# Router logits with the weights stationary, and the last batch of cross-attention interleaved with its output projections, in a Flamingo block kernel on Trainium2

## The chip, the cores and the metric

The kernel runs on one core of a Trainium2 chip. TensorE (PE) multiplies matrices, VectorE (DVE) and ScalarE (ACT) do elementwise work, GpSimd (POOL) does a little of it and issues the DMAs with computed addresses, SyncE (SP) issues the other DMAs. Each engine works off its own queue in order and meets the others only through semaphores. The metric is the time of one execution on the device in microseconds (us); lower is better. The kernel before takes 1012.65 us, the median of three runs (1010.91 to 1013.94).

## What is computed

Eight sequences of 112 tokens (896 tokens, 512 features) pass through four stages, each on a layernorm of x and added to x with a tanh gate:

```
x += tanh(g_xattn[0]) * softmax cross-attention over a context of 8 x 375 rows,
                        output projected with Wo, scaled, layernormed again (gamma, beta)
x += tanh(g_ffn[0])   * (silu(h @ gate.T * gate_s) * (h @ up.T * up_s)) @ down.T * down_s      # inner size 1408
x += tanh(g_xattn[1]) * linear attention: (q kv_summary) / (q k_sum) * sigmoid gate, @ Wo.T
# mixture of experts; t is the layernorm of x
scores = softmax(t @ gate_w.T)            # 16 experts
weights, indices = top_k(scores, 2)
y = sum over experts of swiglu(t; w1[e], w3[e], w2[e]) * weight       # inner size 352
z = swiglu(t; sw1, sw3, sw2)                                          # shared, inner size 704
x += tanh(g_ffn[1]) * (y + z)
```

## The kernel before

**Products.** Operands are split into a high and a low part in a rounded float32 type, and `product` (lines 536 to 543) issues three matmuls for each of the four chunks of 128 features: high by high (L540), high by low (L541), low by high (L542). So one projection of 128 tokens on 512 features is 12 matmuls with 512 moving columns, and one `gate_up` of half the tokens is 12 matmuls with 448. The high part of an operand is a copy by ACT, the low part a subtraction by DVE. The few plain float32 products (L620, L801, L900, L908, L932) each appear in the trace as two matmul instructions.

**First attention, batch by batch.** For each batch b of the loop, PE computes scores for four groups of heads (L603), values (`values_0`), the keys and values of the second attention (`keys_1`, `values_1`), the mix of probabilities and values (L620) and `kv_summary` (L589). DVE clips the scores (`clip`, L1382), ACT exponentiates them (`exps`), DVE normalises the mix (`normalise`, L1389 to L1395) and splits the result into hT (`heads_low`, L1399). The next score product on PE waits for the clip before it, since both use the same PSUM banks. For batches 0 to 6 the tile `k1` lies over the tiles 4 to 6 of x; so after the last `kv_summary`, SP loads these three tiles of x again (`x_again`), and POOL then adds the beta row to them (L1744).

**The last batch** (line 740 on) is written out by hand, with the output projections of the seven token tiles put between its pieces: `to_tokens(t, output_of_0)`, called y0 to y6 here. y0 to y5 need batches 0 to 6 only, y6 needs batch 7 (`ct_sv`). In order PE runs: scores 0, three values_0, scores 1, keys_1 0, y0, mix 0, values_1 0, scores 2, keys_1 1, y1, mix 1, values_1 1, y2, scores 3, keys_1 2, mix 2, values_1 2, y3, mix 3, kv_summary, y4, y5, y6, transposes of tiles 0 to 3 for the first feed-forward, and the first gate_ups with the transposes of tiles 4 to 6 between them. For each projected tile DVE runs `delta` (L1442 to L1446: scale, bias, statistics), ACT a square root (`delta_std`), DVE `residual` (L1452 to L1455 and the statistics L1282 to L1283), ACT a square root (`ln`), DVE `ln_norm` (L1287, L1294), PE the transposes (L642), ACT `ln_save` (L1008) and DVE `ln_low` (L1301).

**The router.** After the second attention PE runs gate_ups of the shared expert's chunk 0 on the first token half, then the last transposes, then `gate_up(1, sh13[1], P, 0, 0)`, then the logits. These are for each of 7 token tiles 12 matmuls with the tokens (128 x 128) stationary and 16 router columns moving, 84 in all, into PSUM bank 1. Then come five more gate_ups of chunks 0 and 1. DVE waits for `lg_mm` with nothing else in hand, subtracts the row maximum (`lg_max`), waits for ACT's exponential (`lg_exp`), and runs softmax, top-2 and the one-hot tables (L1600 to L1625) before `hidden` of chunk 0 (L1516). PE's gate_ups of chunk 2 write the PSUM banks that this `hidden` reads, so they wait for it (`ff_h`, MC + 1). Behind chunk 5 come the ranks (L900, L901), DVE's tables, POOL's scatter of the token rows to DRAM (L1785), the shared down projection (L908) and the loop over sorted tiles of the experts (L932, L942).

Of the kernel before, what the change touches and what calls it, by code (L numbers as in the profile page):

```python
# [20 lines left out]
F32 = mybir.dt.float32  # L21
F32R = mybir.dt.float32r
# [37 lines left out]
def flamingo(nc, x_in, ctx_in, mask_in, cols_in, rows_in, scal_in, wq0_in, wk0_in, wv0_in, wo0_in,  # L60
             gu0_in, wd0_in, wq1_in, wg1_in, wkv1_in, wo1_in, gate_in, sh13_in, sh2_in,
             e13_in, e2_in, out):
    with ExitStack() as stack:
# [30 lines left out]
        gate_r = sb("gate_r", [P, 2, KC * NE], F32R)  # L94
# [92 lines left out]
        k1 = nc.alloc_sbuf_tensor_at("k1", [P, TC, D], F32, offset=x_base + 4 * RT_AT * D)[0:TP]  # L187
        probs = [at(A_P + i * TC * HG * S, HG, TC * S, rows_=TP) for i in range(2)]
# [51 lines left out]

        RT = NT * NE
# [116 lines left out]
        filled = sem("filled")  # L358
        lg_mm = sem("lg_mm")
        lg_max = sem("lg_max")  # L360
        lg_exp = sem("lg_exp")
        lg_sv = sem("lg_sv")
# [68 lines left out]
        def _(sp):  # L431
# [24 lines left out]

            sp.wait_ge(kT_mm, 4 * B)
# [7 lines left out]
            for m in range(2, 9):  # L465
                sp.dma_start(gu0[m][2], gu0_in[m]).then_inc(gu0_ld[m], 16)
            sp.wait_ge(kv_mm, B)
            sp.dma_start(x[:, RT_AT:NT, :], x_in.rearrange("(t p) d -> p t d", p=P)[:, RT_AT:NT, :]).then_inc(x_again, 16)
# [61 lines left out]
        def _(pe):  # L530
# [50 lines left out]
            def kv_summary(b):  # L581
# [3 lines left out]
                for g in range(G):  # L585
                    for c in range(TC):
                        for h in range(HG):
                            at_head = 4 * g + h
                            last = mm(ps[h * HD:(h + 1) * HD, 4, g * (HD + 1):(g + 1) * (HD + 1)],  # L589
                                      k1[:, c, at_head * HD:(at_head + 1) * HD], v1[:, c, at_head, :],  # L590
# [33 lines left out]
            def ln_transposes(n):  # L624
# [8 lines left out]
                elif n < 2 * NT:  # L633
                    if t >= 4:
                        pe.wait_ge(ln_T, (NT + 2, NT + 4, NT + 5)[t - 4])
# [74 lines left out]
            def to_tokens(n, product_of):  # L710

                if 1 <= n < 4 or n == 5:
                    pe.wait_ge(y_sv, n if n < 4 else 4)
                elif n >= NT and n % NT >= 2:
                    pe.wait_ge(y_sv, n - 1)
# [55 lines left out]
            pe.wait_ge(normed, 2 * B)  # L771
            pe.wait_ge(y_sv, NT)
            pe.wait_ge(ln_T, NT + 4)
            pe.wait_ge(gu_low, 1)
            gate_up(0, gu0[0], P, 0, 0)
            gate_up(0, gu0[0], P, 0, 1)
            ln_transposes(NT + 4)
            pe.wait_ge(gu_low, 2)
            gate_up(1, gu0[1], P, 0, 1)
            ln_transposes(NT + 5)  # L780
            ln_transposes(NT + 6)
            gate_up(1, gu0[1], P, 0, 0)
# [83 lines left out]

            pe.wait_ge(ln_T, 3 * NT + 4)
# [5 lines left out]
            pe.wait_ge(y_sv, 3 * NT)  # L873
            pe.wait_ge(gu_low, MC + 2)
# [93 lines left out]
        def _(act):  # L968
# [82 lines left out]
            for i in range(8):  # L1051
# [13 lines left out]
                if i == 5:  # L1065
                    act.wait_ge(gate_ld, 16)
                    fn(gate_r[:, 0, :], gate_w[:], ACT.Copy).then_inc(w_high, 1)
# [28 lines left out]
            keys_1(b, 0)  # L1096
            values_1(b, 0)
            exps(b, 2)
            keys_1(b, 1)
            values_1(b, 1)  # L1100
            delta_std(0)
            fn(warm[:, 0:1], eps[:], ACT.Exp)
            exps(b, 3)
            keys_1(b, 2)
            feed_high(0, gu0[0], gu0_ld[0])
            delta_std(1)
            delta_std(2)
            ln(NT)
            values_1(b, 2)
            feed_high(1, gu0[1], gu0_ld[1])  # L1110
            ln(NT + 1)
            heads_save(b)
            delta_std(3)
            ln(NT + 2)
            delta_std(4)
            delta_std(5)
            ln(NT + 3)
            for t in range(4):
                ln_save(NT + t)
            delta_std(6)  # L1120
            for t in range(4, NT):
                ln(NT + t)
            for t in range(4, NT):
                ln_save(NT + t)
# [73 lines left out]
            ln_save(4 * NT - 1)  # L1198
            act.wait_ge(lg_max, 1)
# [43 lines left out]
        def _(dve):  # L1243
# [122 lines left out]
            def keys_1(b, c):  # L1366
                dve.wait_ge(k1_exp, b * 3 + c + 1)
                v.tensor_scalar(k1[:, c, :], ps[0:TP, 4, :], 0.0, None, ALU.max).then_inc(k1_relu, 1)  # L1368

                dve.wait_ge(k1_relu, b * 3 + c + 1)  # L1370
                v.scalar_tensor_tensor(k1[:, c, :], kexp, 1.0, k1[:, c, :], ALU.min, ALU.add).then_inc(k1_sv, 1)
# [30 lines left out]
            for b in range(B - 1):  # L1402
                if b == 0:
# [5 lines left out]
                    v.tensor_tensor(gate_r[:, 1, :], gate_w[:], gate_r[:, 0, :].bitcast(F32), ALU.subtract  # L1409
# [472 lines left out]
```

## Time and profile before

| | |
|---|---|
| median of three runs | 1012.65 us |
| the profiled execution | 1014.06 us, its span 1012.4 us |
| PE matmul busy | 956.3 us (94%) |
| DVE busy | 465.4 us (46%) |
| ACT busy | 275.9 us (27%) |
| granted TensorE clock, mean | 0.974 |
| chain that ended last, by engine | PE 83%, DVE 8%, DMA 3%, ACT 2% |

The page gives the share of each engine, the granted clock in 40 slices and the chain of work that ended last; the waits say who waited for whom; the timeline gives every instruction with its start, its duration and, in square brackets, the idle time before it and what ended it. Matmuls are pipelined: the duration of one overlaps the next, so the cost of a row of them is taken from the distance of their starts. Two stretches are looked at here: the last batch up to the start of the feed-forward's third chunk (365 to 460 us) and the router (700 to 820 us).

### The profile page before, as it was taken

What the parts mean: (1) busy time and instruction counts of PE and PEld (TensorE: products, weight loads), DVE (VectorE), ACT (ScalarE), POOL (GpSimd) and SP (SyncE); (2) the same over time, 40 slices, a digit from 0 to 9 for tenths busy, and PEclk for the clock granted to TensorE, in tenths of its full rate; (3) what the DMA queues carried; (4) which work ended last, traced back from release to release, by engine and by line L of the source; (5) the groups of instructions that cost most, each with busy time, mean ns of one, the idle gap of its engine ahead of it and who ended that gap; (6) DMA issues with size and microseconds to landing.
All of it is one profiled execution on the core that took longest, in us unless ns stands there. A gap on an engine that the chain in (4) does not pass through costs nothing.

```text
span 1012.4 us, 17141 instructions
## 1 busy us (share of the span) xinstructions
PE 956.3 (94%) x7151; PEld 732.9 (72%) x7152; DVE 465.4 (46%) x751; ACT 275.9 (27%) x424; POOL 82.2 (8%) x111
## 2 busy tenths in 40 slices
PE   5999999999999999889999999989999989999991
PEld 5878788887878787679997447977996446566550
DVE  6664555454554465962220446977322311222224
ACT  4533333333333334232111114332210021121210
POOL 0000000000000010100000003120000502222111
PEclk9999999999999999879999999999799999999996
DMA  8100010010100020430003005513402317977726
GB/s 323 31 2 32 2 32 32 1 33 1 74 2 32 1 84 2 178 155 1 1 1 125 1 0 215 201 58 110 148 1 86 147 43 244 330 250 247 265 69 232
DMA packets 26770, 95.99 MB, mean 95 GB/s; under 512 B 3282, under 2 KB 4306, under 8 KB 23634
## 3 DMA queue, kind: packets, MB, share of 16 engines
q1 hardware_dynamic: 20354, 72.69, 20.2%
q0 software_dynamic: 6352, 22.35, 6.2%
q8 instruction: 52, 0.85, 0.4%
q14 instruction: 12, 0.10, 0.0%
HBM read 76.37 MB, written 18.66 MB: 94 GB/s over the span
## 4 chain that ended last, share of the span: by engine, by line
PE 83%; DVE 8%; DMA 3%; ACT 2%; issue 2%; POOL 1%; SPq 0%; POOLq 0%; DVEq 0%; ACTq 0%
PE ps L540 17%; PE ps L541 16%; PE ps L542 16%; PE ps L932 10%; PE ps L801 7%; PE ps L942 5%; PE ps L620 4%; PE ps L603 3%; PE ps L821 1%; POOL sorted_rows L1785 1%; PE ps L923 1%; DVE arena L1294 1%; DMA land_c<-in_ctx 1%; DVE stats L1282 1%; PE ps L949 1%
## 5 line engine op out<-in xcount | busy, mean ns | idle before, releaser
L540 PE MATMUL ps<-arena_r 128*125 128x512 f32 (+1 forms) x416 | 164.3, 395 | 4.2 <-DVE arena_r L1260 4.2
L541 PE MATMUL ps<-arena_r 128*125 128x512 f32 (+1 forms) x416 | 157.3, 378 | 0.0
L542 PE MATMUL ps<-arena_r 128*125 128x512 f32 (+1 forms) x416 | 157.1, 378 | 0.0
L540 PE MATMUL ps<-hT,arena_r 128*128 128x448 f32 (+1 forms) x368 | 138.2, 376 | 3.5 <-DVE hT L1301 3.3
L541 PE MATMUL ps<-hT,arena_r 128*128 128x448 f32 (+1 forms) x368 | 136.4, 371 | 0.0
L542 PE MATMUL ps<-hT,arena_r 128*128 128x448 f32 (+1 forms) x368 | 136.3, 370 | 0.0
L932 PE MATMUL ps<-arena 128*128 x336 | 103.1, 460 | 1.8 <-ACT arena L1216 1.0
L996 ACT ACTIVATE arena<-arena,mbias,mscale 125x448 f32<-125x448 f32 x96 | 66.1, 752 | 106.1 <-DVE arena L1382 106.1
L540 PEld LDWEIGHTS ps<-arena_r 128*125 128x125 f32 (+1 forms) x416 | 78.3, 188 | 21.9 <-DVE arena_r L1260 4.6
L542 PEld LDWEIGHTS ps<-arena_r 128*125 128x125 f32 (+1 forms) x416 | 78.2, 188 | 13.7
L932 PEld LDWEIGHTS ps<-arena 128*128 128x128 f32 x336 | 62.3, 190 | 33.3 <-issue 2.2
L541 PEld LDWEIGHTS ps<-arena_r 128*125 128x125 f32 (+1 forms) x416 | 78.4, 188 | 10.6
L540 PEld LDWEIGHTS ps<-hT,arena_r 128*128 128x128 f32 (+1 forms) x368 | 69.9, 190 | 10.6 <-issue 3.9
L542 PEld LDWEIGHTS ps<-hT,arena_r 128*128 128x128 f32 (+1 forms) x368 | 69.6, 189 | 6.6
L541 PEld LDWEIGHTS ps<-hT,arena_r 128*128 128x128 f32 (+1 forms) x368 | 69.8, 190 | 6.2
L801 PE MATMUL ps<-arena 128*128 128x512 f32 x154 | 66.9, 592 | 0.0
L1382 DVE TENSOR_SCALAR arena<-ps 125x1344 f32<-125x1344 f32 x32 | 49.8, 1557 | 22.5 <-PE ps L603 22.2
L942 PE MATMUL ps<-arena 128*128 (+1 forms) x126 | 57.9, 595 | 1.7 <-DVE arena L1691 1.2
L801 PEld LDWEIGHTS ps<-arena 128*128 128x128 f32 x154 | 29.0, 190 | 34.4 <-issue 34.4
L1516 DVE SCALAR_TENSOR_TENSOR arena<-ps,cols,arena 128x896 f32<-128x896 f32 x11 | 12.7, 1151 | 77.3 <-ACT arena L1132 77.3
L620 PEld LDWEIGHTS ps<-arena 125*32 125x32 f32 x1536 | 35.8, 110 | 12.4 <-issue 12.0
L1368 DVE TENSOR_SCALAR k<-ps 125x512 f32<-125x512 f32 x24 | 16.6, 692 | 60.1 <-ACT arena L985 60.1
(197 smaller groups left out, 1172.6 us busy)
## 6 DMA issues: line engine op xcount, KB each, us to landing
arena<-in_e SPq DMA_DIRECT2D x16, 1408.0 KB, 6.8
arena<-in_e SPq DMA_DIRECT2D x16, 512.0 KB, 7.5
sorted_rows<-arena POOLq DMA_DIRECT2D x1, 7453.0 KB, 24.2
land_c<-in_ctx SPq DMA_DIRECT2D x8, 752.0 KB, 4.3
arena<-sorted_rows POOLq DMA_DIRECT2D x21, 257.0 KB, 5.4
land_w<-in_gu SPq DMA_DIRECT2D x8, 512.0 KB, 4.5
arena<-token_rows SPq DMA_DIRECT2D x14, 256.0 KB, 4.7
arena<-in_e SPq DMA_DIRECT2D x16, 192.0 KB, 9.6
```

The costliest lines, as they stand in the source:

```text
L540: mm(into, a[0], w[0], start=i == 0, stop=False)
L541: mm(into, a[0], w[1], start=False, stop=False)
L542: last = mm(into, a[1], w[0], start=False, stop=i == len(operands) - 1)
L603: last = mm(ps[0:TP, h, c * S:(c + 1) * S], kT[key_half][r, g, c * TP:(c + 1) * TP], queries[query_half][r, b, g, :], start=i == 0, stop=i ...
L620: last = mm(ps[h * HD:(h + 1) * HD, 7, first:first + S], w, probs[g % 2][:, h, c * S:(c + 1) * S], start=c == 0, stop=c == TC - 1)
L801: last = mm(into, h0[m][:, t * P:(t + 1) * P], wd0[:, m, :], start=m == 0, stop=m == MC - 1)
L932: last = mm(ps[:, 4 + j, 0:EI], xgT[:, k, :], arena[:, bass.ds(w + (k * 2 * EI + j * EI), EI)], start=k == 0, stop=k == KC - 1)
L942: last = mm(ps[:, 3, :], hmoeT[0:z, c, :], arena[0:z, bass.ds(w + (2816 + c * D), D)], start=c == 0, stop=c == 2)
L996: done = fn(p, p, ACT.Exp, bias=mbias[:, b * 3 + c:b * 3 + c + 1], scale=mscale[:, b * 3 + c:b * 3 + c + 1])
L1368: v.tensor_scalar(k1[:, c, :], ps[0:TP, 4, :], 0.0, None, ALU.max).then_inc(k1_relu, 1)
L1382: v.tensor_scalar(probs[g % 2], ps[0:TP, 0:HG, 0:TC * S], -CLIP / SCALE, CLIP / SCALE, ALU.max, ALU.min).then_inc(clipped, 1)
L1516: v.scalar_tensor_tensor(into[0:size].rearrange("p (n t) -> p n t", n=2), ps[0:size, 4 * (1 - m % 2) + 2:4 * (1 - m % 2) + 4, 0:HALF], sca ...
```

## The change

**Router.** `gate_r` is laid out as [chunk, high or low, expert]. A new function `logits_T` makes the router weights the stationary side: for each chunk one matmul with 32 stationary columns (16 high, 16 low) and the high part of 448 tokens moving, and one with the 16 high columns and the low part of the tokens moving; 8 matmuls for half of the tokens, two halves, into banks 1 and 3. ACT copies each result (32 x 448) to SBUF (`lgT`). Seven small plain float32 products follow, with 128 tokens of `lgT` stationary (32 rows) and a 32 x 16 matrix `pair` of two stacked identities moving, which transpose and add high and low rows at once. They lie behind the two gate_ups of chunk 0 on the second half. The last two gate_ups of chunk 1 change places, and the last one waits for `lg_max` where it waited for `lg_sv` (behind the exponential). POOL builds `pair` once at the start.

**Last batch.** The k1 of the last batch lies in the context area (`k1_last`), and SP reloads the x tiles after kv_summary of batch 6 in place of batch 7. SP loads chunks 6 to 8 of the feed-forward weights after the last kv_summary. All projections use bank 6, and each waits for the delta before it. The projections and the transposes are moved ahead in PE's order, and DVE's and ACT's orders are rewritten to match: DVE finishes each tile (residual, ln_norm) soon after its delta, and ACT has two more changes of function table.

```diff
         def ln_bank(n):
             if NT <= n < 2 * NT:
-                return (0, 1, 2, 3, 1, 3, 1)[n - NT]
+                return (0, 1, 2, 3, 0, 1, 3)[n - NT]
         def y_bank(n):
-            return (6, 6, 6, 6, 5, 6, 4)[n] if n < NT else n % 2
+            return 6 if n < NT else n % 2
...
+            sp.wait_ge(kv_mm, B - 1)
+            sp.dma_start(x[:, RT_AT:NT, :], x_in.rearrange("(t p) d -> p t d", p=P)[:, RT_AT:NT, :]).then_inc(x_again, 16)
             sp.wait_ge(kT_mm, 4 * B)
...
             to_tokens(0, output_of_0)
             mix(b, 0)
             values_1(b, 0)
+            to_tokens(1, output_of_0)
             scores(b, 2)
             keys_1(b, 1)
-            to_tokens(1, output_of_0)
+            to_tokens(2, output_of_0)
             mix(b, 1)
             values_1(b, 1)
-            to_tokens(2, output_of_0)
+            to_tokens(3, output_of_0)
             scores(b, 3)
             keys_1(b, 2)
+            to_tokens(4, output_of_0)
+            pe.wait_ge(clipped, 4 * B)
+            ln_transposes(NT)
             mix(b, 2)
+            ln_transposes(NT + 1)
             values_1(b, 2)
-            to_tokens(3, output_of_0)
+            to_tokens(5, output_of_0)
+            ln_transposes(NT + 2)
             mix(b, 3)
+            ln_transposes(NT + 3)
             kv_summary(b)
-            to_tokens(4, output_of_0)
-            to_tokens(5, output_of_0)
-            pe.wait_ge(kv_sv, B)
+            ln_transposes(NT + 4)
             to_tokens(6, output_of_0)
-            pe.wait_ge(clipped, 4 * B)
-            for t in range(4):
-                ln_transposes(NT + t)
...
+            def logits_T(n):
+                into = ps[:, 1 + 2 * n, 0:HALF]
+                for k in range(KC):
+                    mm(into[0:2 * NE], gate_r[:, k, :, :].rearrange("p j e -> p (j e)"), piece(hT, k, n * HALF, HALF)[0],
+                       start=k == 0, stop=False)
+                    last = mm(into[0:NE], gate_r[:, k, 0, :], piece(hT, k, n * HALF, HALF)[1],
+                              start=False, stop=k == KC - 1)
+                last.then_inc(lg_mm, 1)
...
             pe.wait_ge(y_sv, 3 * NT)
+            logits_T(0)
             pe.wait_ge(gu_low, MC + 2)
             gate_up(1, sh13[1], P, 0, 0)
             pe.wait_ge(ln_T, 4 * NT)
-            for t in range(NT):
-                last = product(ps[:, 1, t * NE:(t + 1) * NE],
-                               [(tok(hT, k, t), (gate_r[:, 0, k * NE:(k + 1) * NE], gate_r[:, 1, k * NE:(k + 1) * NE]))
-                                for k in range(KC)])
-            last.then_inc(lg_mm, 1)
+            logits_T(1)
             gate_up(0, sh13[0], P, 1, 0)
             gate_up(0, sh13[0], P, 1, 1).then_inc(ff_mm, 1)
+            pe.wait_ge(consts_set, 2)
+            pe.wait_ge(lgT_sv, 2)
+            for t in range(NT):
+                last = mm(ps[:, 1, t * NE:(t + 1) * NE], lgT[:, t * P:(t + 1) * P], pair[:], start=True, stop=True)
+            last.then_inc(lg_mm, 1)
             gate_up(1, sh13[1], P, 0, 1)
-            pe.wait_ge(lg_sv, 1)
-            gate_up(1, sh13[1], P, 1, 0)
-            gate_up(1, sh13[1], P, 1, 1).then_inc(ff_mm, 1)
+            gate_up(1, sh13[1], P, 1, 1)
+            pe.wait_ge(lg_max, 1)
+            gate_up(1, sh13[1], P, 1, 0).then_inc(ff_mm, 1)
...
@@ DVE, last batch: the new order @@
+            clip(b, 1); keys_1(b, 0); delta(0); residual(0); ln_norm(NT); delta(1); clip(b, 2); feed_low(0, gu0[0])
+            keys_1(b, 1); residual(1); ln_norm(NT + 1); delta(2); residual(2); normalise(b, 0); ln_norm(NT + 2)
+            delta(3); clip(b, 3); feed_low(1, gu0[1]); keys_1(b, 2); residual(3); delta(4); ln_low(NT)
+            ln_norm(NT + 3); residual(4); ln_low(NT + 1); ln_norm(NT + 4); delta(5); ln_low(NT + 2)
+            normalise(b, 1); heads_low(b); ln_low(NT + 3); residual(5); kv_save(b); ln_norm(NT + 5)
+            ln_low(NT + 4); delta(6); residual(6); ln_low(NT + 5); ln_norm(NT + 6); ln_low(NT + 6)
```

(The last block writes on six lines what stands on one line each in the code; the lines that it replaces are in the listing of the kernel before.)

## Rows read from the trace of the kernel before

**Rows 1.** The page: busy us, share of the span, instructions.
```profile
PE 956.3 (94%) x7151; PEld 732.9 (72%) x7152; DVE 465.4 (46%) x751; ACT 275.9 (27%) x424; POOL 82.2 (8%) x111
```

**Rows 2.** The waits of PE: who waited for whom, us in total, times, longest.
```profile
PE ps L642 <- DVE arena L1294: 13.4, 5, 7.2
PE ps L540 <- DVE hT L1399: 3.3, 1, 3.3
```

**Rows 3.** Timeline of PE, the router: start us, us, engine, line, names, shape.
```profile
710.30 0.17 PE L540 MATMUL ps<-gate_r,hT 128*128 128x16 f32 x1
...
714.80 0.36 PE L542 MATMUL ps<-gate_r,hT 128*128 128x16 f32 x1
...
723.97 0.72 PE L540 MATMUL ps<-hT,arena_r 128*128 128x448 f32 x1
...
728.54 0.37 PE L540 MATMUL ps<-hT,arena_r 128*128 128x448 f32 x1
...
738.27 0.36 PE L540 MATMUL ps<-hT,arena_r 128*128 128x448 f32 x1
```

**Rows 4.** Timeline of PE, small float32 products elsewhere.
```profile
777.25 0.37 PE L900 MATMUL ps<-arena 128*128 128x112 f32 x2
...
403.74 1.36 PE L620 MATMUL ps<-arena 125*32 125x112 f32 x48
```

**Rows 5.** Timeline of DVE, the router, in brackets idle before and releaser.
```profile
724.15 0.28 DVE L1600 TENSOR_REDUCE arena<-ps 128x7 f32<-128x112 f32 x1 [14.64 <-PE ps L542]
...
733.67 1.09 DVE L1516 SCALAR_TENSOR_TENSOR arena<-ps,arena 128x896 f32<-128x896 f32 x1
```

**Rows 6.** Timeline of PE: three restarts after 3 us of idleness.
```profile
422.09 0.77 PE L540 MATMUL ps<-arena_r,hT 128*128 128x512 f32 x1 [3.31 <-DVE hT L1399]
...
435.86 0.71 PE L540 MATMUL ps<-hT,arena_r 128*128 128x448 f32 x1 [3.06 <-DVE hT L1301]
...
676.18 0.47 PE L540 MATMUL ps<-arena_r,hT 128*128 128x512 f32 x1 [3.39 <-DVE hT L1563]
```

**Rows 7.** Windows: stretch, length, busy of five engines, PE clock, DMA, GB/s.
```profile
422.00:424.00 2.00, 1.91 (x5) 1.56 (x6) 1.93 (x3) 0.00 (x0) 1.34 (x2) 0.50 0.04 9
...
428.00:430.00 2.00, 1.19 (x10) 0.95 (x8) 1.93 (x4) 0.30 (x1) 0.00 (x0) 0.98 0.00 0
```

**Rows 8.** Timeline of PE, the first gate_ups of the feed-forward.
```profile
459.41 0.37 PE L540 MATMUL ps<-hT,arena_r 128*128 128x448 f32 x1
```

**Rows 9.** Timeline of DVE, the last batch.
```profile
399.71 0.75 DVE L1442 SCALAR_TENSOR_TENSOR arena<-ps,rs,arena 128x512 f32<-128x512 f32 x1 [2.62 <-PE ps L542]
...
401.32 1.52 DVE L1382 TENSOR_SCALAR arena<-ps 125x1344 f32<-125x1344 f32 x1
402.76 0.15 DVE L1452 RECIPROCAL drstd<-dstd 128x1 f32<-128x1 f32 x1
...
405.46 0.69 DVE L1368 TENSOR_SCALAR k<-ps 125x512 f32<-125x512 f32 x1
...
411.73 0.15 DVE L1287 RECIPROCAL rstd<-std 128x1 f32<-128x1 f32 x1
...
412.38 0.75 DVE L1442 SCALAR_TENSOR_TENSOR arena<-ps,rs,arena 128x512 f32<-128x512 f32 x1
...
416.56 0.36 DVE L1389 TENSOR_SCALAR zinv<-ps 128x224 f32<-128x224 f32 x1
...
419.27 0.28 DVE L1377 TENSOR_SCALAR arena<-ps 128x128 f32<-128x128 f32 x1
```

**Rows 10.** Timelines of POOL and DVE: the beta rows and DVE beside them.
```profile
422.66 4.19 POOL L1744 TENSOR_TENSOR x<-x,arena 128x512 f32<-128x512 f32 x3 [41.47 <-DMA x<-in_x]
...
422.84 1.65 DVE L1455 SCALAR_TENSOR_TENSOR x<-arena,drstd,x 128x512 f32<-128x512 f32 x1
```

**Rows 11.** Timeline of ACT, the last batch: a table load and what follows.
```profile
397.54 1.28 ACT L1091 ACT_TABLE_LOAD   x1
398.84 0.30 ACT L1091 ACTIVATE dstd<-dmv,eps 128x1 f32<-128x1 f32 x1
```

More of the change, by code:

```diff
@@ L93, in flamingo @@
         gate_w = sb("gate_w", [P, KC * NE])
-        gate_r = sb("gate_r", [P, 2, KC * NE], F32R)
+        gate_r = sb("gate_r", [P, KC, 2, NE], F32R)
+        pair = sb("pair", [2 * NE, NE])
         dest = sb("dest", [P, 2, NT], U32)
@@ L1066, in _ @@
                     act.wait_ge(gate_ld, 16)
-                    fn(gate_r[:, 0, :], gate_w[:], ACT.Copy).then_inc(w_high, 1)
+                    fn(gate_r[:, :, 0, :], gate_w[:].rearrange("p (k e) -> p k e", k=KC), ACT.Copy).then_inc(w_high, 1)
             act.wait_ge(mask_set, 2)
@@ L1096, in _ @@
             keys_1(b, 0)
+            delta_std(0)
+            ln(NT)
             values_1(b, 0)
+            fn(warm[:, 0:1], eps[:], ACT.Exp)
+            feed_high(0, gu0[0], gu0_ld[0])
             exps(b, 2)
             keys_1(b, 1)
+            delta_std(1)
+            ln(NT + 1)
+            delta_std(2)
             values_1(b, 1)
[L1101 to L1102 removed]
+            ln(NT + 2)
+            fn(warm[:, 1:2], eps[:], ACT.Exp)
+            feed_high(1, gu0[1], gu0_ld[1])
             exps(b, 3)
             keys_1(b, 2)
[L1105 to L1108, printed above, removed]
+            delta_std(3)
+            ln_save(NT)
+            ln(NT + 3)
+            ln_save(NT + 1)
+            delta_std(4)
             values_1(b, 2)
[L1110 to L1111 removed]
+            ln(NT + 4)
+            ln_save(NT + 2)
             heads_save(b)
[L1113 to L1115 removed]
+            ln_save(NT + 3)
             delta_std(5)
[L1117 to L1119 removed]
+            ln_save(NT + 4)
+            ln(NT + 5)
             delta_std(6)
[L1121 to L1124, printed above, removed]
+            ln_save(NT + 5)
+            ln(NT + 6)
+            ln_save(NT + 6)
             for m in range(MC):
@@ L1198, in _ @@
             ln_save(4 * NT - 1)
+            for n in range(2):
+                act.wait_ge(lg_mm, n + 1)
+                fn(lgT[:, n * HALF:(n + 1) * HALF], ps[0:2 * NE, 1 + 2 * n, 0:HALF], ACT.Copy).then_inc(lgT_sv, 1)
             act.wait_ge(lg_max, 1)
@@ L1472, in _ @@
             delta(0)
+            residual(0)
+            ln_norm(NT)
+            delta(1)
             clip(b, 2)
+            feed_low(0, gu0[0])
             keys_1(b, 1)
-            delta(1)
+            residual(1)
+            ln_norm(NT + 1)
+            delta(2)
+            residual(2)
             normalise(b, 0)
-            delta(2)
+            ln_norm(NT + 2)
+            delta(3)
             clip(b, 3)
-            residual(0)
+            feed_low(1, gu0[1])
             keys_1(b, 2)
-            residual(1)
-            feed_low(0, gu0[0])
-            ln_norm(NT)
-            delta(3)
-            residual(2)
+            residual(3)
+            delta(4)
+            ln_low(NT)
+            ln_norm(NT + 3)
+            residual(4)
+            ln_low(NT + 1)
+            ln_norm(NT + 4)
+            delta(5)
+            ln_low(NT + 2)
             normalise(b, 1)
+            heads_low(b)
+            ln_low(NT + 3)
+            residual(5)
             kv_save(b)
-            ln_norm(NT + 1)
-            feed_low(1, gu0[1])
-            heads_low(b)
-            residual(3)
-            ln_norm(NT + 2)
-            delta(4)
-            delta(5)
-            ln_norm(NT + 3)
-            ln_low(NT)
-            ln_low(NT + 1)
-            delta(6)
-            ln_low(NT + 2)
-            ln_low(NT + 3)
-            residual(4)
-            residual(5)
-            ln_norm(NT + 4)
-            residual(6)
             ln_norm(NT + 5)
             ln_low(NT + 4)
+            delta(6)
+            residual(6)
+            ln_low(NT + 5)
             ln_norm(NT + 6)
-            ln_low(NT + 5)
             ln_low(NT + 6)
```

47 lines of the change are left out of this document (29 added, 18 removed).

## Prediction

> **What bounds the kernel now.** The page comes first: PE is busy 94% of the span [rows 1], and the chain that ended last is PE for 83%. So what can be gained is PE work that isn't needed, PE's waits, and PE time at the lower clock. The waits come next: where PE waits, it waits for DVE, for normalised tiles and for the last heads of the batch [rows 2]. The timelines then show where. At 422.09 PE begins again after 3.31 us of waiting for heads_low of batch 7, and at 435.86 after 3.06 us of waiting for ln_low [rows 6]. The window from 422 stands at a granted clock of 0.50, 1.2 of 2.4 GHz, and the one from 428 is back [rows 7]. In the router the 84 logit matmuls last from 710.30 to 723.97, 13.67 us; 41 of them take 0.110 us each and the other 43 0.213 us, the clock having fallen at 714.80 in the middle of them, with PE never idle. The gate_ups behind still run slowly up to 728.54 [rows 3].
>
> **The router: PE's own time.** The 60 gate_up matmuls between the logits and chunk 2 take 14.30 us (723.97 to 738.27), of which 48 at full clock take 9.73, or 0.203 each [rows 3]. Of the new order, the 16 matmuls of logits_T stream 448 columns as those do, and I price them at 0.203: 3.24 us. Their stationary side is 32 or 16 columns wide, which no row shows; the streaming sets the pace of the 448-column rows, so a smaller load shouldn't lengthen them. The seven small products are 14 instructions. Above, the 16-column logits at the lower clock bound them: 0.213; below, the 48 instructions of L620 in 1.29 us, 0.027 each, which share the array in four parts [rows 4]; the two of L900 with 112 columns take 0.105 each, and the 16-column logits at full clock 0.110 [rows 3]. The last is nearest (128 stationary columns, 16 moving): 1.54 us, between 0.4 and 3.0. ACT's two copies of lgT lie beside 24 gate_up matmuls (4.88 us), and a PSUM copy of this width takes ACT about 0.6 us, so PE doesn't wait for them. So from 710.30, had PE nobody to wait for: 3.24 + 60 x 0.203 + 1.54 = 16.96, chunk 2 at 727.3 and not 738.27. That is 11.0 us of PE time.
>
> **The router: what comes late next.** Chunk 2 also waits for DVE's hidden of chunk 0, and DVE reaches it only behind the whole top-2 chain. From the start of L1600 at 724.15 to the end of that hidden (733.67 + 1.09) are 10.6 us [rows 5]; before, this ended 3.5 us ahead of PE and cost nothing. In the new order the small products end at 710.30 + 3.24 + 4.88 + 1.54 = 720.0, DVE begins at about 720.2, and hidden ends at 730.8. PE stands ready at 727.3 and begins chunk 2 at 730.95: a wait of 3.6 us takes the place of a third of the gain. In the rows, three waits of 3.1 to 3.4 us each stand beside a stretch at 0.50 [rows 6, 7], and the slow stretches end 4.4 to 5.9 us after PE restarted (428.0 after 422.09; 728.3 after 723.97). For 448-column matmuls a slow one takes 0.373 in place of 0.203 (4.57 us for 12, [rows 3]), so each slow microsecond loses 0.46: 1.5 to 2.7 us, and I take 2.1. The router then gives 738.27 - 730.95 - 2.1 = 5.2 us, 7.3 if the clock holds. Everything behind is pushed forward as a block: the gate_ups of chunks 2 to 5 run without a gap, and the ranks, the scatter, the down projection and the expert loop each hang on their end.
>
> **The last batch: DVE is the bound.** I walked all four queues item by item: each item starts when the one ahead of it is done and what it waits for is done, 0.05 us per hand-over (0.13 to PE). Prices are distances of starts: delta 1.61, clip 1.44, residual 2.70 (402.76 to 405.46), ln_norm 0.65, normalise 2.71 [rows 9]; keys_1 1.35, feed_low 1.11 and ln_low 0.6 from the same timeline; a square root on ACT with both hand-overs 0.42; a projection 2.87, scores 1.12, mix 1.29, a tile's transposes 0.40, a gate_up 2.44. The same walk of the old order gives heads_low at 421.93 (the row behind it: 422.09) and chunk 2 of the feed-forward at 457.4. The trace has 459.41 [rows 8]; the 2.0 us between lie in two DVE instructions beside POOL's late beta rows, of which one stood 1.65 us where its like take 0.75 [rows 10].
>
> In the new order DVE, from its first delta at 383.3 to heads_low, has six deltas, five residuals, five ln_norms, two clips, two keys_1, two feed_lows, two normalises, three ln_lows and heads_low: 9.7 + 13.4 + 3.3 + 2.9 + 2.7 + 2.2 + 5.4 + 1.8 + 0.5 = 41.9 us, and waits of 5.9 (four square roots 1.7, the exponentials of the keys 2 x 1.6, the copy of the heads 0.7, the rest small). Heads_low ends at 431.1, 9 us later than before. PE meanwhile waits 1.6, 1.2 and 2.1 us ahead of y3, y4 and y5, and 5.8 us ahead of y6. y6 starts at 431.25, at the lower clock (12 x 0.427 = 5.1 and a start), and ends at 436.5. But then the other tiles are ready: four gate_ups with two sets of transposes run to 447.4, and the last tile's ln_low (delta, residual, ln_norm, transposes, save, low behind y6) is there at 446.4, one microsecond ahead of its need. Four more gate_ups, and chunk 2 starts at 457.15. Gain 459.4 - 457.15 = 2.25 us.
>
> **Edits at nothing.** The x tiles land some 60 us earlier on a queue that otherwise waits, and POOL's beta rows move to 381 to 385, where DVE waits for ACT; if that cover fails, up to 0.9. Without this move the 2.0 us above would stay. The last gate_up's wait for lg_max is met 3 us before. Building pair lies beside the first loads. Chunks 6 to 8 of the weights have more than 30 us until their use.
>
> The Trainium skill (GPSIMD Engine Reference, Specifications) says that GpSimd's SBUF interfaces are shared with VectorE and that it contends with instructions that have two SBUF inputs; the slow L1455 has two of them, and the trace agrees. By that rule too the earlier reload is worth the 2.0 us.
>
> **Sum.** 5.2 + 2.25 = 7.4 us. The profiled execution took 1014.06 (span 1012.4) and becomes 1006.6. It lies 1.4 above the median of the runs; I put the gain on the median: 1012.65 - 7.4 = 1005.2.
>
> **Rivals.** (a) The clock holds through the router's new wait, or that wait is shorter because the small products cost less: 2.1 to 3 us more gain, 1002 to 1003. For it: only the moment of the wait decides, and it is barely 3.6 us. Against it: all three waits above 3 us have slow stretches. Chance 0.2.
> (b) The last batch gives nothing or costs 1 to 3 us: DVE's new queue alternates with ACT at some twenty places, and 0.1 per hand-over in place of 0.05 moves chunk 2 from 457.15 to 458.0, 0.15 to 459.0. 1007 to 1010. For it: PE's early waits are new. Chance 0.22.
> (c) PE is better covered than I walk it (hand-overs to DVE cheaper, no fall of the clock at y6, 2 us): with (a), 996 to 1001. Chance 0.12.
> (d) The other side: the short waits of 1.2 to 2.1 us, with work between them, bring the clock down from the first of them (399.5) and keep it there until the gate_ups are dense. Walked so, with PE at half clock from 401 for 20 us and again from y6, chunk 2 starts at 466.6, 7.2 us later than before, and the whole takes 1012.65 - 5.2 + 7.2 = 1014.7. It decides at about 14 slow us (461.4, a loss of 2.0); to be slower by over 0.3% it must also hold in the router's new order. For it: the clock fell in the logits with PE never idle [rows 3]. Against it: the projections between the waits are dense. Chance 0.06.
> (e) ACT's changes of table, five before the last tile where there were three, cost twice what they show: the walk then gives 460.3, chunk 2 is 0.9 later than before, the total 1008.3. The rows speak against it: the load takes 1.28 and the next instruction starts 0.02 after its end [rows 11]. Chance 0.03. The Trainium skill (ScalarE: Activation LUTs, What ACT_TABLE_LOAD costs) puts a switch at about 2.66 us with a drain; by that rule it would be this case, and the trace doesn't agree here.
> (f) The change doesn't do what it says: the logits stay a PE cost, because the narrow stationary side slows the stream to its low-clock pace (16 x 0.373 and 14 x 0.213, 4.2 us more, part of it ahead of DVE's chain). 1009 to 1010. Chance 0.05.
>
> **How the numbers follow.** The forecast, 1003.5 to 1007, has 0.32. Its own range with (a), (b), (e) and most of (f) covers 1000 to 1010, which I give as the range; outside it are most of (c) and (d). About 0.3% (3 us) is what a measurement of this kernel can tell from no change. Faster by more than that, below 1009.6: 0.87 (all but a part of (b) and (f), and (d)). Within: 0.10. Slower, above 1015.7: 0.03.
>
> **What would show it.** After: 16 matmuls gate_r by hT with 448 columns at 0.20 each and 14 small ones at about 0.11; L1600's equivalent starting some 4 us after its old place in the order, without 14 us of idleness; a wait of 3 to 4 us of PE on DVE's hidden ahead of chunk 2, with a slow stretch behind it; chunk 2 of the feed-forward at about 457; heads_low at about 431 with PE waiting 5 to 6 us for it; POOL's beta rows in one piece before 386. Wrong would be: no wait ahead of shared chunk 2 (then the gain there is 11), or a feed-forward that starts later than 459.

## The result and the profile after

The changed kernel takes 1006.49 us (median of 15 runs, 1003.06 to 1010.69), the kernel before, run beside it, 1012.65 (15 runs, 1010.45 to 1015.37). The ratio is 0.994, with a 95% interval from 0.9926 to 0.9954: 6.1 us faster. The forecast was 7.4 us, to 1005.2. The profiled execution took 1005.44 us (span 1003.8) where the one of before took 1014.06. Of the executions below one, of small_x4 (1217.54 us at a mean granted clock of 0.747), ran in a slower state and is left out of that run's median and ratio.

The page of after, busy us, share of the span, instructions (beside [rows 1]):

```profile
PE 947.0 (94%) x7097; PEld 720.1 (72%) x7098; DVE 466.0 (46%) x751; ACT 280.1 (28%) x429; POOL 82.2 (8%) x112
```

PE's sum fell by 9.3 us, but durations overlap, so the pitches of the timelines carry the reading. Router, after, PE (start us, us, engine, line, names, shape, in brackets idle before and releaser):

```profile
706.10 0.45 PE L883 MATMUL ps<-hT,gate_r 128*32 128x448 f32 x1
...
707.80 0.36 PE L549 MATMUL ps<-hT,arena_r 128*128 128x448 f32 x1
...
710.24 0.37 PE L883 MATMUL ps<-hT,gate_r 128*32 128x448 f32 x1
710.44 0.36 PE L885 MATMUL ps<-hT,gate_r 128*16 128x448 f32 x1
...
711.87 0.36 PE L549 MATMUL ps<-hT,arena_r 128*128 128x448 f32 x1
...
716.83 1.73 PE L907 MATMUL ps<-pair,arena 32*128 32x16 f32 x14
718.49 0.47 PE L549 MATMUL ps<-hT,arena_r 128*128 128x448 f32 x1
...
729.35 0.47 PE L549 MATMUL ps<-hT,arena_r 128*128 128x448 f32 x1 [3.16 <-DVE arena L1550]
729.62 0.56 PE L550 MATMUL ps<-hT,arena_r 128*128 128x448 f32 x1
...
733.21 0.36 PE L551 MATMUL ps<-hT,arena_r 128*128 128x448 f32 x1
```

The logits were 84 matmuls in 13.67 us [rows 3]; now they are twice 8 in 1.7 us each and 14 small ones in 1.66 (716.83 to 718.49). Chunk 2 (729.35) has a wait of 3.16 us ahead of it that it didn't have [rows 3], and 3.4 us behind the restart run at the pitch of the lower clock (0.373 in place of 0.203). DVE, after, shows what PE waits for:

```profile
718.59 0.27 DVE L1634 TENSOR_REDUCE arena<-ps 128x7 f32<-128x112 f32 x1 [10.73 <-PE ps L907]
...
728.11 1.09 DVE L1550 SCALAR_TENSOR_TENSOR arena<-ps,arena 128x896 f32<-128x896 f32 x1
```

From the row maximum to the end of hidden are again 10.6 us [rows 5]. The last batch: waits of PE in it and the start of the feed-forward's chunk 2 (PE, after):

```profile
400.18 0.50 PE L549 MATMUL ps<-arena_r,hT 128*128 128x512 f32 x1 [2.07 <-DVE arena L1476]
...
408.20 0.50 PE L549 MATMUL ps<-arena_r,hT 128*128 128x512 f32 x1 [0.89 <-DVE arena L1476]
...
430.40 0.76 PE L549 MATMUL ps<-arena_r,hT 128*128 128x512 f32 x1 [3.81 <-DVE hT L1432]
...
456.27 0.36 PE L549 MATMUL ps<-hT,arena_r 128*128 128x448 f32 x1
```

The first two stand ahead of y3 and y4, the third ahead of y6; y5 has one of 1.78 at 418.13. The last line is the start of chunk 2.

**Where the 8.6 us between the two profiled executions went.** I cut both at four points, into five stretches. Batch 7 (its first score products) starts at 363.26 in place of 364.83: 1.57, since the first big wait of PE was 2.9 us and not 4.2, in code that the change doesn't touch; the twelve executions below have it between 362.7 and 364.1. From there to chunk 2 of the feed-forward: 94.58 before, 93.01 after, 1.57 gained. From there to the first gate_up of the router: 242.58 before, 244.07 after, 1.5 lost. The router, up to the first expert product (818.20 and 810.68): 116.21 and 110.34, 5.87 gained. The rest, 1.1 gained. The three stretches with unchanged code add up to 1.2 us, so the medians (6.1) and the two edited stretches (7.4) agree to within this scatter.

### The profile page after: what moved, and what is told of

Its sections match the earlier page's. It is cut to its first block, busy times and chain, and to the rows that moved or that the text cites. A ratio compares the mean times of both kernels' runs of the same rounds, so it can differ in the third digit from the quotient of the medians.

```text
span 1003.8 us, 17041 instructions
## 1 busy us (share of the span) xinstructions
PE 947.0 (94%) x7097; PEld 720.1 (72%) x7098; DVE 466.0 (46%) x751; ACT 280.1 (28%) x429; POOL 82.2 (8%) x112
## 4 chain that ended last, share of the span: by engine, by line
PE 81%; DVE 9%; ACT 3%; DMA 3%; issue 2%; POOL 1%; SPq 0%; POOLq 0%; DVEq 0%; ACTq 0%
PE ps L549 17%; PE ps L550 15%; PE ps L551 15%; PE ps L956 10%; PE ps L813 7%; PE ps L966 5%; PE ps L629 4%; PE ps L612 3%; PE ps L833 1%; POOL sorted_rows L1822 1%; DVE stats L1314 1%; PE ps L947 1%; PE ps L973 1%; DMA token_rows<-arena,to_row 1%; PE ps L651 1%
## 5 line engine op out<-in xcount | busy, mean ns | idle before, releaser
L1714 DVE SCALAR_TENSOR_TENSOR arena<-ps,arena 128x352 f32<-128x352 f32 x21 | 12.3, 584 | 71.0 <-PE ps L956 43.8
```

Of the source, the lines that this page charges most:

```text
L1714: v.scalar_tensor_tensor(hmoe[:, 0:EI], ps[:, 5, 0:EI], weight, smoe, ALU.mult, ALU.mult).then_inc(m_h, 1)
```

## The experiments

Below, "batch" is the distance from the first score products of batch 7 to chunk 2 of the feed-forward (94.58 before, 93.01 after), "router" the distance from its first gate_up to the first expert product (116.21, 110.34). Ratios are to the kernel before on the same chip, intervals 95%.

### One part alone

**router_only** has the router's hunks of the diff, **batch_only** the others, **after_base** is the changed kernel again.

```diff
 # router_only: logits_T, lgT, pair, the small products; batch_only: all the rest
```

> The kernel before with the router's part of the change alone (logits_T, the small products, the gate_up order); the last batch is as before. My theory (PE saves 11 us, a wait on DVE's hidden takes 3 to 4 back, the clock 1 to 2 more): 5 to 6 us faster than before, about 1007, with a wait of 3.2 us ahead of the shared expert's chunk 2. Rival, the router as a pure PE saving with nothing late behind it: 11 us faster. Rival, the last batch carries the gain: under 2 us faster.

> The kernel before with the last batch's part of the change alone; the router is as before. My theory: heads_low 9 us later, yet the feed-forward's third chunk about 1.6 us earlier than in the kernel before, counted from the scores of the last batch; 1 to 2.5 us faster in time. Rival, the new order is worth nothing: 0. Rival, the two parts need each other: the two single gains would not add to the whole (6 us).

> The changed kernel itself, for comparison with the others on one chip: 6 to 7 us faster than before. It also tells how much of the difference of single profiles is the start (first PE wait 2.9 or 4.2 us) and the clock ahead of the second attention.

| | median us | ratio | batch | router | wait ahead of chunk 2 |
|---|---|---|---|---|---|
| router_only | 1007.17 | 0.9945 [0.9927, 0.9963] | 94.06 | 110.16 | 3.30 |
| batch_only | 1011.47 | 0.9988 [0.9974, 1.0003] | 93.10 | 115.76 | none |
| after_base | 1005.48 | 0.9935 [0.9914, 0.9957] | 91.77 | 110.79 | 3.31 |

The router carries the gain (5.6 of 6.6 us by the ratios); the batch part alone can't be told from no change by its time, though its stretch is 1.5 us shorter. The two ratios add up to 6.8 us, so nothing speaks for the rival that the parts need each other, within intervals of nearly 2 us each way.

### Is the top-2 chain what PE waits for?

**hidden_first**: as after, but DVE does hidden of chunk 0 ahead of the softmax and the top-2 chain.

```diff
             v.memset(hmoe[:, EI:3 * P], 0.0)
             feed_low(MC + 2, sh13[2])
+            hidden(MC, 0, P, 1.0, silu1[0], hsh[0])
...
-                hidden(MC + m, m, size, 1.0, silu1[m % 2], hsh[m])
+                if m > 0:
+                    hidden(MC + m, m, size, 1.0, silu1[m % 2], hsh[m])
```

> The changed kernel, with DVE's hidden of the shared chunk 0 put ahead of the top-2 chain in place of behind it. My theory, that the chain on DVE holds PE's chunk 2 back: the wait of 3.2 us disappears and with it the slow stretch of 3.4 us behind it (1.2 to 1.5 us); 4 to 4.5 us faster than the changed kernel. Rival, something else is late next (the weight split feed_low, the silu of chunk 1, the scatter chain further on): 0 to 2 us. Rival, the clock falls there by itself after the small products: about 3 us.

1002.11 us, ratio 0.9889 [0.9864, 0.9914]; router 105.68, no wait ahead of chunk 2. DVE of hidden_first:

```profile
723.52 1.09 DVE L1550 SCALAR_TENSOR_TENSOR arena<-ps,arena 128x896 f32<-128x896 f32 x1 [1.08 <-ACT arena L1240]
```

Counted from the router's first gate_up, hidden starts 5.3 us earlier than in after (22.45 and 27.77), and the router is 4.7 shorter, more than the wait of 3.16: the slow stretch behind the wait went too (no window from 700 to 745 is below a clock of 1.00), so the clock hadn't fallen for the small products.

**small_earlier**: as after, with the small products one gate_up earlier, ahead of `gate_up(0, sh13[0], P, 1, 1)`.

```diff
             gate_up(0, sh13[0], P, 1, 0)
-            gate_up(0, sh13[0], P, 1, 1).then_inc(ff_mm, 1)
             pe.wait_ge(consts_set, 2)
             pe.wait_ge(lgT_sv, 2)
             ...
             last.then_inc(lg_mm, 1)
+            gate_up(0, sh13[0], P, 1, 1).then_inc(ff_mm, 1)
```

> The changed kernel, with the seven small products one gate_up earlier (behind the first gate_up of chunk 0 on the second token half). DVE's chain theory: DVE begins 2.4 us earlier, PE's wait ahead of chunk 2 goes from 3.2 to 0.7 us, and without a wait of 3 us the clock doesn't fall: 3.5 us faster than the changed kernel. If the clock falls for the thin products and not for the wait: 2.4 us. Rival, PE's own queue is the bound: 0.

1001.19 us, ratio 0.9884 [0.9869, 0.9899]; router 106.08. PE of small_earlier:

```profile
712.64 1.73 PE L906 MATMUL ps<-pair,arena 32*128 32x16 f32 x14
...
725.17 0.44 PE L549 MATMUL ps<-hT,arena_r 128*128 128x448 f32 x1 [0.69 <-DVE arena L1550]
```

PE's work is the same. The chain starts one gate_up (2.44 us) earlier, the wait shrinks by 2.5, and the router by 4.3 (3.5 was expected): behind the wait of 0.69 the clock stays at 1.00.

**small_x4**: as after, each small product issued four times (56 instructions); the repeats write the same values.

```diff
-            for t in range(NT):
+            for t in range(4 * NT):
+                t = t % NT
```

> The changed kernel with each of the seven small products done four times (56 instructions in place of 14). It measures their price and whether they bring the clock down: at 0.11 us each the stretch lasts 6.2 us, and DVE's chain and so chunk 2 come 4.6 us later, one for one, though PE had 3.2 us of idleness there: 4.6 us slower than the changed kernel. If PE's time and not DVE's chain decided: 1.4 us slower. If the clock falls within them as it did within the 16-column logits, 1 to 2 us more.

1012.06 us (seven executions), ratio 0.9978 [0.9954, 1.0002]; router 115.38, 5.0 more than after. PE of small_x4, then its windows (stretch, length, busy of five engines, PE clock, DMA share, GB/s):

```profile
718.60 7.25 PE L908 MATMUL ps<-pair,arena 32*128 32x16 f32 x56
725.78 0.74 PE L549 MATMUL ps<-hT,arena_r 128*128 128x448 f32 x1
...
736.65 0.44 PE L549 MATMUL ps<-hT,arena_r 128*128 128x448 f32 x1 [1.01 <-DVE arena L1551]
```

```profile
722.00:724.00 2.00, 2.00 (x21) 2.00 (x20) 0.00 (x0) 0.00 (x0) 0.00 (x0) 1.00 0.00 0
724.00:726.00 2.00, 2.00 (x11) 1.96 (x11) 0.11 (x1) 0.00 (x0) 0.00 (x0) 0.50 0.00 0
```

The block took 7.2 us, 5.5 more than 14 instructions did: 4.7 would be 42 more at 0.112; the remaining 0.8 is what ran after the clock had fallen, inside the block, with PE busy throughout. Chunk 2 starts 34.54 us behind the router's first gate_up where in after it was 29.01: 5.5 more, although PE's own work behind the block became slower and its wait shrank to 1.01. So the delay goes one for one onto chunk 2, since DVE's chain hangs on the block. At the first expert product 5.0 of the 5.5 are left, because here no slow stretch follows behind chunk 2. By the ratios the whole is 3.8 us slower than after (0.9978 and 0.994, give or take 2.8); the expectation of 4.6 with 1 to 2 for the clock lies within that, but so do the 1.4 of PE's own time, so it is the trace that decides between them.

### What the last batch's gain is made of

**reload_only**: the kernel before with k1 of batch 7 in the context area, x reloaded one batch earlier and the weights of chunks 6 to 8 loaded later; all orders as before. These are three edits at once (the first is needed for the second); they weren't timed one by one.

```diff
+            sp.wait_ge(kv_mm, B - 1)
+            sp.dma_start(x[:, RT_AT:NT, :], ...).then_inc(x_again, 16)
...
-            for m in range(2, 9):
+            for m in range(2, 6):
...
-            sp.dma_start(x[:, RT_AT:NT, :], ...).then_inc(x_again, 16)
+            for m in range(6, 9):
+                sp.dma_start(gu0[m][2], gu0_in[m]).then_inc(gu0_ld[m], 16)
```

> The kernel before with one thing of the last batch's part: k1 of the last batch lies in the context area and the x tiles are loaded again 58 us earlier, all orders as before. My theory, that POOL's late beta rows hold two DVE instructions for 2.0 us that PE then waits for: 1.5 to 2 us faster than before. Rival, those 2 us lie beside other waits: 0.

1011.66 us, ratio 0.9985 [0.9976, 0.9995]; batch 92.06. So the time falls by 1.5 us and the stretch by 2.5, with the old order and its three waits. Up to y6 nothing changes (57.26 and 57.25 us behind the first score products); the whole gain lies behind it, where POOL's late beta rows stood. Two DVE instructions there were held by 0.90 [rows 10] and 1.07, 2.0 together, and in reload_only they aren't. The other 0.5 is within the scatter: router_only, whose last batch is that of before, has 94.06 for 94.58. DVE of before, then of reload_only:

```profile
425.51 1.62 DVE L1294 TENSOR_SCALAR arena<-x,mv,rstd 128x512 f32<-128x512 f32 x1
```

```profile
421.20 0.75 DVE L1463 SCALAR_TENSOR_TENSOR x<-arena,drstd,x 128x512 f32<-128x512 f32 x1
...
422.98 0.55 DVE L1301 TENSOR_SCALAR arena<-x,mv,rstd 128x512 f32<-128x512 f32 x1
```

The three waits, PE of reload_only:

```profile
420.45 0.47 PE L547 MATMUL ps<-arena_r,hT 128*128 128x512 f32 x1 [3.29 <-DVE hT L1407]
...
428.07 0.66 PE L649 MATMUL ps<-ident,arena 128*128 128x128 f32 x4 [3.29 <-DVE arena L1301]
...
432.24 0.71 PE L547 MATMUL ps<-hT,arena_r 128*128 128x448 f32 x1 [3.52 <-DVE hT L1308]
```

**router_reload**: the router part and reload_only's edit together, that is the changed kernel without the new order of the last batch.

```diff
 # reload_only + the router's hunks of the change
```

> The changed kernel without the new order of the last batch: the router's part and the early reload of the x tiles, with PE's, DVE's and ACT's orders in the last batch as before. Theory, from reload_only: the early reload is the whole gain of the last batch, the new order of the queues is worth 0 to 0.5 us; so this runs as fast as the changed kernel, ratio to the kernel before 0.993 to 0.9945. Rival, the new order carries a gain of its own of 2 us or more: 0.996.

1005.53 us, ratio 0.9919 [0.9904, 0.9935]; batch 92.08, router 110.53. It is no slower than the changed kernel (0.994 and 0.9935; its own ratio lies below the 0.993 to 0.9945 expected, but the intervals overlap), so no gain of the new order is to be seen.

**late_reload**: batch_only with the x tiles reloaded behind the last kv_summary.

```diff
-            sp.wait_ge(kv_mm, B - 1)
-            sp.dma_start(x[:, RT_AT:NT, :], ...).then_inc(x_again, 16)
...
             sp.wait_ge(kv_mm, B)
+            sp.dma_start(x[:, RT_AT:NT, :], ...).then_inc(x_again, 16)
```

> The last batch's part alone (router as before), with the x tiles reloaded after kv_summary of the last batch, as in the kernel before. In the new order DVE reaches residual of tile 4 at about 420, ahead of heads_low, and needs POOL's beta row of tile 4, which needs this load, issued at about 426 and landed 4 to 9 us later. Theory: heads_low comes 9 to 13 us later than in batch_only and the kernel is 8 to 12 us slower than batch_only: the early reload is what allows the new order. Rival, DVE has other work to fill that time: under 3 us.

1020.26 us, ratio 1.0057 [1.0033, 1.0082]: 0.69% of the time, about 7 us (4 to 10), more than batch_only, a little less than the 8 to 12 expected; the traces have 9.7 in this stretch (102.77 and 93.10). DVE of late_reload:

```profile
429.51 1.67 DVE L1470 SCALAR_TENSOR_TENSOR x<-arena,drstd,x 128x512 f32<-128x512 f32 x1 [9.91 <-POOL x L1759]
```

DVE stands 9.9 us at the residual of a late tile, for POOL, which waits for the tiles. heads_low, queued behind, starts 76.1 us behind the first score products in place of 66.4 in batch_only, and PE waits 10.5 and 5.2 us. So the new order needs the early reload.

**fill_y6**: as after, with the first gate_up of the feed-forward ahead of y6 on PE, kv_save and a ln_low ahead of normalise on DVE, and a tile's save ahead of the heads' copy on ACT.

```diff
             ln_transposes(NT + 4)
+            pe.wait_ge(kv_sv, B)
+            pe.wait_ge(ln_T, NT + 4)
+            pe.wait_ge(gu_low, 1)
+            gate_up_0()
             to_tokens(6, output_of_0)
...
             ln_low(NT + 2)
+            kv_save(b)
+            ln_low(NT + 3)
             normalise(b, 1)
             heads_low(b)
-            ln_low(NT + 3)
             residual(5)
-            kv_save(b)
```

> The changed kernel, with the feed-forward's first gate_up put ahead of y6, into PE's wait for heads_low; for that kv_save and ln_low of tile 3 come ahead of normalise on DVE, and ln_save of tile 3 ahead of the copy of the heads on ACT. My theory (the wait of 3.8 us ahead of y6 costs its own length plus the slow clock of y6): 3.5 to 4.5 us faster than the changed kernel, with no window at 0.50 from 430 to 436. Rival, the tail behind y6 (delta, residual, ln_norm, transposes) sets the end of the stretch and y6 comes 0.9 us later: 0 or a loss of up to 1 us.

1003.25 us, ratio 0.9904 [0.9889, 0.9919]; batch 90.73. PE of fill_y6:

```profile
426.65 0.44 PE L549 MATMUL ps<-hT,arena_r 128*128 128x448 f32 x1 [2.18 <-DVE ks L1413]
...
430.69 0.47 PE L549 MATMUL ps<-arena_r,hT 128*128 128x512 f32 x1 [1.33 <-DVE hT L1434]
```

The long wait ahead of y6 (3.81 us in after, 5.38 in after_base) is split in two by one gate_up, the stretch is 2.3 and 1.0 us shorter than in these two, and 1.3 shorter than reload_only's, and y6 starts at full clock; no window from 414 to 446 is below 1.00. By the ratios the gain on the changed kernel is 3.6 us (3.1 on after_base), where 3.5 to 4.5 was expected. Only with this fill does the new order pay, and the case for that is in the traces: 90.7 us in all three executions with the fill, 92.1 in both with the old order and the early reload (reload_only, router_reload). In time fill_y6 can't be told from router_reload (0.9904 and 0.9919, overlapping intervals).

### Together

**merged_best** is small_earlier and fill_y6; **best_mid** is that, with hidden of chunk 0 between the top-8 loop and the tables that follow it.

```diff
+            hidden(MC, 0, P, 1.0, silu1[0], hsh[0])
             then(v.tensor_copy(idxf, idx8[:, :, 0:2]))
```

> The changed kernel with both of the edits that gained alone: the small products one gate_up earlier, and the feed-forward's first gate_up ahead of y6. The two lie 290 us apart and touch different waits, so the theory that each takes its own wait away says that the gains add: ratio to the kernel before about 0.985, 15 us. Rival, they share a bound behind the router: no more than the better of the two, 0.988.

> As merged_best, and DVE's hidden of the shared chunk 0 stands in the middle of the router's chain (behind the top-8 loop). The 0.7 us wait ahead of chunk 2 that small_earlier left should go: 0.5 to 0.7 us more than merged_best, at the edge of what can be measured; the trace should show no wait there.

| | median us | ratio | batch | router | wait ahead of chunk 2 |
|---|---|---|---|---|---|
| merged_best | 1000.75 | 0.9865 [0.9842, 0.9888] | 90.73 | 106.64 | 0.69 |
| best_mid | 999.19 | 0.9856 [0.9835, 0.9878] | 90.75 | 105.81 | none |

best_mid is the fastest, 14 us ahead of the kernel before and 7 to 8 ahead of the changed one. merged_best's interval holds both the 0.985 of gains that add and the rival's 0.988, so the times don't decide between them; in its trace the stretches are as short, or nearly so, as with each edit alone (90.73 and 90.73, 106.64 and 106.08). The step from merged_best to best_mid is too small for the times as well; the trace shows the wait gone and the router 0.8 us shorter. Its windows over the router (columns as above):

```profile
715.00:720.00 5.00, 5.00 (x26) 4.55 (x25) 3.46 (x16) 4.39 (x5) 0.00 (x0) 1.00 0.13 29
720.00:725.00 5.00, 5.00 (x26) 4.55 (x25) 4.45 (x24) 0.37 (x1) 0.00 (x0) 1.00 0.00 0
725.00:730.00 5.00, 5.00 (x26) 4.54 (x25) 3.08 (x5) 1.28 (x2) 0.00 (x0) 1.00 0.00 0
```

PE is busy all of this time, at the full clock. No wait and no fall is left there.

## Why the prediction was right

**PE's own time in the router: right.** The 16 matmuls of logits_T have the pitch of 0.203 us that I took from the 448-column rows, though their stationary side has 32 or 16 columns. So rival (f) is refuted. The small products took 1.66 us where I said 1.54: 0.112 each and a start. PE's whole saving up to chunk 2 was 10.4 us (7.3 at chunk 2 and the wait of 3.16) and not 11.0; besides those 0.1, the 36 gate_up matmuls behind the small products stand 0.207 apart and not 0.203.

**What comes late next: right.** I forecast a wait of 3.6 us on DVE's hidden; it was 3.16, and 3.31 in after_base and 3.30 in router_only. hidden_first and small_earlier show the mechanism: take the chain off PE's path, and 4.3 to 4.7 us come back with PE's work unchanged. small_x4 shows the other direction.

**The clock: right in kind, 0.6 too dear.** 3.4 us at the lower clock behind the restart lose 3.4 x 0.46 = 1.5 us; I took 2.1. Of the two lengths that it came from, 5.9 and 4.4 us, the second was misread: at 723.97 PE didn't restart, it came out of the logits, with the clock down since 714.80. Chunk 2 starts 7.27 us earlier, counted from the router's first gate_up (36.28 before, 29.01 after), where the walk had 7.3 (738.27 - 730.95): PE's saving and the wait each came out about half a microsecond smaller, which cancels. So the router gave 5.87 and not 5.2 because of the clock term. Rival (a), that the clock would hold, did not come about in any of the five executions with this wait (after, after_base, router_only, router_reload, fill_y6).

**The last batch: 0.7 us too much in this trace.** The walk, moved by the 1.57 us of the earlier start, gives y6 at 429.7 and chunk 2 at 455.6; the trace has 430.40 and 456.27, 0.7 late. The step that failed is "POOL's beta rows move to 381 to 385, where DVE waits for ACT". They ran from 374.20 to 383.8, and held a DVE instruction of keys_1. POOL and DVE of after:

```profile
374.20 9.59 POOL L1781 TENSOR_TENSOR x<-x,arena 128x512 f32<-128x512 f32 x7 [372.21 <-DVE arena L1500]
```

```profile
380.88 1.76 DVE L1404 SCALAR_TENSOR_TENSOR arena<-arena 125x512 f32<-125x512 f32 x1
```

Its like take 0.69, so 1.07 is lost, in after_base and batch_only too. The text had priced that failure at up to 0.9. late_reload settles the cause: it has the same new order, but the beta rows of tiles 4 to 6 come after 428. DVE, then PE of late_reload:

```profile
380.44 0.69 DVE L1386 SCALAR_TENSOR_TENSOR arena<-arena 125x512 f32<-125x512 f32 x1
```

```profile
398.68 0.50 PE L546 MATMUL ps<-arena_r,hT 128*128 128x512 f32 x1 [1.01 <-DVE arena L1457]
```

The wait ahead of y3 is 1.01 in place of 2.07, and DVE comes to the residual of tile 4 at 56.0 us behind the first score products in place of 57.1 in batch_only. So the beta rows cost 1.06 of DVE's chain, and the rest of the walk up to y6 was, by difference, 0.35 too long. Behind y6 the trace of after happens to fit the walk. In all six executions that have the change's last batch y6 starts 67.13 to 67.14 us behind the first score products (the walk: 66.4), but from there to chunk 2 after and batch_only take 25.9 and 26.0, as walked, and the other four (after_base, hidden_first, small_earlier, small_x4) 24.5 to 24.8, the clock having come back earlier. Against the one trace of before the stretch is thus shorter by 1.5 to 2.9 us, where I forecast 2.25.

I also forecast waits of 1.6, 1.2, 2.1 and 5.8 us; they were 2.07, 0.89, 1.78 and 3.81. The last is 5.35 to 5.38 in the other five executions with this last batch; in after alone the clock fell at y5, PE reached the wait later, and y6 started at the same moment.

**Which edit earns it: right, but its price is another.** The text gave the reload 2.0 us (without it "the 2.0 us above would stay") and left 0.25 for the new order (chunk 2 at 457.15 against the old order's walk of 457.4). reload_only gained 2.5 in its trace, 2.0 of it in the two DVE instructions named, and 1.5 (0.5 to 2.4) in time; router_reload is as fast as the changed kernel: the order is worth nothing that can be measured. What PE does earlier in it is paid back in the wait ahead of y6, which starts 9.9 us later than in the old order (67.1 and 57.3 behind the first score products). One thing in the text on this was too narrow: of the two instructions that POOL held, L1455 reads two tensors from SBUF, but L1294 reads one (and two columns of scalars), so the rule on two inputs accounts for 0.9 of the 2.0. The phrase itself fell with late_reload: with the new order and the late reload not 2 us are lost but some 7 (9.7 in the trace), because a residual of a late tile now stands in DVE's queue ahead of heads_low. A reload's moment was priced by the old queue.

**The other rivals.** (d), a clock that stays low from the first short waits on, did not happen: the stretches at half clock were 419 to 422 and 430 to 436. (e) fell: the table load takes 1.28 us again and the next instruction follows at once (ACT, after):

```profile
404.16 0.29 ACT L1026 ACTIVATE std<-mv,eps 128x1 f32<-128x1 f32 x1 [2.27 <-DVE mv L1315]
404.47 1.28 ACT L1133 ACT_TABLE_LOAD   x1
405.76 0.20 ACT L1133 ACTIVATE warm<-eps 128x1 f32<-128x1 f32 x1
```

The 2.66 us of the Trainium skill (ScalarE: Activation LUTs, What ACT_TABLE_LOAD costs) isn't seen here: neither ahead of the load, which starts 0.02 us behind the ACTIVATE before it, nor behind it do these rows leave room for a drain. (b), nothing from the last batch, isn't excluded by batch_only's interval (0.9974 to 1.0003), but the stretch is shorter by 1.5 to 2.9 us in the six executions that have the change's last batch.

**The sum.** 5.9 + 1.6 = 7.4 us in the traces, as forecast, and 6.1 in the medians (interval 4.7 to 7.5). That the traces hit 7.4 is luck: the router gave 0.7 more than its term and the last batch 0.7 less, and with the tail of after_base in place of after's the last batch alone would have given 2.8.

## What to carry to other kernels

When PE work ahead of a chain on another engine is removed, walk that chain to its consumer before counting the gain: here 3.2 of 10.4 us turned into a wait and 1.5 into slow matmuls, and one line that starts the chain a gate_up earlier, or lets the consumer's operand be made first, gave back more than the last-batch rewrite did. When an edit has a precondition (a buffer moved, a transfer made earlier), time the precondition alone: it may be the whole gain. A wait that brings the clock down costs more than its length: here 3.16 us cost 1.5 more, and shortening it by 2.5, to 0.69, gave 4.3.

## What the runs showed that I had not expected

- The clock fell with PE never idle, under matmuls with 16 moving columns. In small_x4 the granted clock was 1.00 up to 724 and 0.50 from there, 5.4 us into a block of matmuls with 16 moving columns, and came back at 731. In before it fell 4.5 us into the logits [rows 3], in reload_only 3.3 us. In after's block of 1.66 us it held.
- The clock differs between executions of the same code. After's waits of 2.07, 0.89 and 1.78 us ended in a fall at y5, and those of after_base, 2.07, 0.82 and 1.75, did not; behind y6 the stretch at half clock ended near 436 in after and near 433.5 in after_base, 1.2 us of difference in "batch". Windows of after, then of after_base:

```profile
420.00:422.00 2.00, 2.00 (x6) 1.52 (x6) 1.89 (x5) 0.00 (x0) 0.00 (x0) 0.50 0.96 379
...
434.00:436.00 2.00, 2.00 (x6) 1.60 (x5) 1.25 (x3) 0.00 (x0) 0.00 (x0) 0.50 0.00 0
```

```profile
420.00:422.00 2.00, 2.00 (x19) 1.53 (x21) 1.93 (x4) 0.10 (x1) 0.00 (x0) 1.00 0.94 369
...
434.00:436.00 2.00, 2.00 (x11) 1.74 (x10) 1.89 (x4) 0.04 (x1) 0.00 (x0) 1.00 0.00 0
```

- So a difference of 1 to 3 us between two single traces says little: the stretch between chunk 2 of the feed-forward and the router, the same code in all kernels, took from 242.3 to 246.4 us in the fourteen profiled executions.
- A DVE instruction with two SBUF inputs beside POOL took 1.76 us where it takes 0.69 alone (L1404), and the residual L1470 of late_reload 1.67 against 0.75. The Trainium skill (GPSIMD Engine Reference, Specifications) names contention between GpSimd and such instructions, and these traces agree, with 0.9 to 1.1 us for 512 columns. But L1294 of before, with one tensor from SBUF, was held as well, 1.62 in place of 0.55.
